# A recurrent cell with a mixture of experts: error rows from transposed predictions, the second hidden state in one operation, history entries and history products moved

## The chip, the cores and the metric

The kernel runs on one core of one Trainium2 chip. The metric is the time on the device, in microseconds (us), of one execution. The core's engines run side by side, each through its own list of instructions, and meet only at semaphores: TensorE (PE, with its weight loads as PEld), VectorE (DVE), ScalarE (ACT), GpSimd (POOL) and SyncE (SP), which here only issues DMA transfers.

## The reference

2048 sequences of 256 steps go through a recurrent cell. A step needs the state, the error and the memory that earlier steps left, so the steps follow one another.

```python
encoded = tanh(xt @ We + st @ Ue + be)                    # 24 values
new_state = tanh(xt @ Wx[c] + st @ Ws[c] + bk[c])         # 8 candidates of 32 values
mem = concatenate([[encoded, err], mem[:, :-1]])          # the 20 last entries of 25 values
a = relu(mem.reshape(b, -1) @ enc_w1 + enc_b1)            # 64
agent_in = relu(a @ enc_w2 + enc_b2)                      # 16
h1, c1 = lstm_cell(agent_in, h1, c1, ...)                 # 16
h2, c2 = lstm_cell(h1, h2, c2, ...)
gate = softmax(h2 @ gate_w + gate_b)                      # 8
theta = clamp01(mean(abs(mem[:, :10, -1])) * 2.5)         # of the 10 last errors
gate = gate * theta + gs * (1 - theta)
st = sum over c of gate[c] * new_state[c]
pred = clamp01(st[:, -1]); err = pred - yt                # pred is the output
```

## The kernel before

The 2048 sequences are two groups of 1024 (8 tiles of 128). An item is one step of one group, so there are 512 items, taken in turn: group 0, group 1, group 0 of the next step, and so on. An item's successor in its own group is two items later. `run_phases` (line 162) writes, for every engine, one phase an item: two phases ahead of the loop, 51 turns of 10 phases (5 steps of both groups, 510 phases), two behind it. A phase of an engine works on three items: `new`, `cur` (the one before) and `old` (two before). The order in which an engine's `phase` function calls its parts is its order of instructions; nothing else sets it.

What one phase of each engine does:

- TensorE (line 447). The memory product (`a_ps`) is the largest part: 12 pairs of `history` matmuls (line 359; a pair is the two column halves of the array, run beside each other) for the older entries, in four steps `kk` of three `PIECES`, spread over two phases so that they lie between parts that wait. `history_waits` (line 352) waits until the entry of the group's last step is in `hist`. Then `state_transpose` (line 289, tiles of 128x128), `encoded_s` (313), `logit_bias` and `gate_logits` (422, 430), `encoder1_now` (371: the newest entry straight from `entry`), `bias_of_cell` (393), `encoder2` (382), `candidates_bias` (324), `cell_gates` of cell 0 (406), `candidates_x` and `candidates_s` (333, 342), `encoded_x`, and `cell_gates` of cell 1, which waits for cell 0's h.
- ScalarE (line 588): all tanh and exponentials, the copy of the transposed state out of PSUM (`state_take`), the relu of the error rows (`at_least_zero`, 520), the fp16 high part of the entry (`entry_high`, 526), copies of h (`next_hidden`, 574).
- VectorE (line 832): cell arithmetic (`cell_terms`, `cell_value`, `new_hidden`), softmax, `mix` and `mix_sum` (the weighted sum over the candidates), `errors` (710), `prediction` (820).
- GpSimd (line 964): `gate_in_sbuf`, two quarters of the mix (`mix_quarter`, 911), kept share of the gate, `new_error`, `keep_prediction`, and `entry_low` (923), the fp16 low part of the entry.
- SyncE (line 240): when both parts of the entry of an item are made (semaphore `q_el`, added to by `entry_low`), four DMAs, one for each quarter q, copy `entry_parts` into `hist` (line 271). Every second phase it also fetches history weights, x and y ahead of need.

An entry's way into `hist` is therefore: `encoded_s` on TensorE, tanh and `entry_high` on ScalarE, `entry_low` on GpSimd, four DMAs, and `history_waits` on TensorE one phase later. The error rows reach `entry` by a unit column in `w_ue`: TensorE multiplies the state into rows 96 to 99, ScalarE takes the relu, VectorE the minimum with 1 and the difference from y.

## Time and profile before

| | us |
|---|---|
| median of 3 runs | 5462.91 |
| lowest, highest | 5460.96, 5463.51 |
| the profiled execution, its own time | 5460.57 |
| its span in the profile | 5458.7 |

| engine | busy us | share of the span |
|---|---|---|
| PE | 5391.8 | 99% |
| PEld | 3426.0 | 63% |
| DVE | 4479.8 | 82% |
| ACT | 3807.2 | 70% |
| POOL | 2421.7 | 44% |

The granted clock of TensorE is at its full level (2.4 GHz) in all 40 slices, and all slices look alike, so one phase out of the middle stands for the others. Matmuls are pipelined: a row of the timeline shows each from its start to the end of its results, so neighbours overlap. The chain of waits shows them end to end, which is what adds up to a phase. PE at 99% means that a matmul is always under way, not that the array is never held up between two forms of work.

### The profile page before, as it was taken

How to read it: one execution, taken by the hardware profiler on the slowest of the kernel's cores; microseconds unless marked ns; L12 is line 12 of the kernel's file. 1: busy time of each engine (PE TensorE's matmuls, PEld its weight loads, DVE VectorE, ACT ScalarE, POOL GpSimd, SP SyncE). 2: the span in 40 equal slices, each digit the busy share in tenths (PEclk: the TensorE clock that was granted, in tenths of full speed). 3: DMA queues.
4: the chain of work that ended last, by engine and by line, in shares of the span. 5: the costliest groups of instructions: out<-in, count | busy, mean ns of one | idle time of the engine just before them, and what ended most of it. 6: DMA issues, size and time to landing. Idle time of an engine off the chain costs nothing.

```text
span 5458.7 us, 188210 instructions
## 1 busy us (share of the span) xinstructions
PE 5391.8 (99%) x67584; PEld 3426.0 (63%) x67584; DVE 4479.8 (82%) x12336; ACT 3807.2 (70%) x9729; POOL 2421.7 (44%) x4613
## 2 busy tenths in 40 slices
PE   8999999999999999999999999999999999999998
PEld 5666666666666666666666666666666666666665
DVE  7888888888888888888888888888888888888887
ACT  5777777777767777777777777777777777777775
POOL 3444444444444444444444444444444444444444
PEclk9999999999999999999999999999999999999999
DMA  2111111111111111111111111111111111111111
GB/s 69 29 29 32 29 32 29 32 29 32 29 32 29 32 29 30 31 29 32 29 32 29 32 29 32 29 32 29 30 31 29 32 29 32 29 32 29 32 29 40
DMA packets 299285, 172.38 MB, mean 32 GB/s; under 512 B 156734, under 2 KB 263882, under 8 KB 298714
## 3 DMA queue, kind: packets, MB, share of 16 engines
q1 hardware_dynamic: 293568, 159.42, 11.2%
q8 instruction: 564, 9.24, 0.7%
q10 hardware_dynamic: 5146, 3.66, 0.2%
q14 instruction: 7, 0.06, 0.0%
HBM read 74.65 MB, written 2.10 MB: 14 GB/s over the span
## 4 chain that ended last, share of the span: by engine, by line
PE 95%; DVE 4%; issue 1%; DMA 0%; POOL 0%; ACT 0%; DVEq 0%; ACTq 0%; POOLq 0%
PE a_ps L366 26%; PE chain L417 17%; PE cand_ps L338 9%; PE a_ps L377 9%; PE cand_ps L347 7%; PE chain L310 5%; PE chain L317 4%; PE chain L403 4%; PE chain L293 4%; PE a_ps L388 3%; PE chain L435 3%; PE cand_ps L330 3%; DVE mixed L799 1%; DVE state L817 1%; DVE added L720 1%
## 5 line engine op out<-in xcount | busy, mean ns | idle before, releaser
L366 PE MATMUL a_ps<-hist,w_hist 125*64 125x512 f16 x12288 | 1896.3, 383 | 24.1 <-DMA w_hist<-enc_table 24.1
L817 DVE TENSOR_REDUCE state<-mixed 128x64 f32<-128x512 f32 x2048 | 1353.4, 682 | 34.2 <-POOL mixed L920 0.8
L920 POOL TENSOR_TENSOR mixed<-cand,gate 128x512 f32<-128x512 f32 x1024 | 1281.1, 1272 | 48.6 <-POOL gate L908 12.5
L554 ACT ACTIVATE cand<-cand_ps 128x512 f32<-128x512 f32 x2048 | 1101.8, 593 | 91.1 <-PE cand_ps L347 90.6
L417 PE MATMUL chain<-cell_in,cell_w 128*64 128x128 f32 x16384 | 1120.7, 278 | 19.8 <-DVE cell_in L735 19.8
L886 POOL TENSOR_TENSOR one_theta<-ones,theta 128x8 f32<-128x8 f32 x512 | 103.4, 202 | 2241.0 <-DVE theta L702 2241.0
L417 PEld LDWEIGHTS chain<-cell_in,cell_w 128*64 128x64 f32 x16384 | 889.2, 136 | 271.5 <-DVE cell_in L735 211.8
L366 PEld LDWEIGHTS a_ps<-hist,w_hist 125*64 125x64 f16 x12288 | 681.4, 109 | 536.2 <-issue 141.7
L561 ACT ACTIVATE gates<-chain 128x384 f32<-128x384 f32 x1024 | 502.0, 490 | 726.3 <-PE chain L417 726.1
L735 DVE SCALAR_TENSOR_TENSOR cell_in<-gates,tanh_c 64x128 f32<-64x128 f32 x2048 | 582.5, 284 | 127.0 <-ACT tanh_c L571 113.4
L720 DVE SCALAR_TENSOR_TENSOR added<-gates 128x256 f32<-128x256 f32 x1024 | 537.1, 524 | 141.2 <-ACT gates L561 141.2
L799 DVE TENSOR_TENSOR mixed<-cand,chain 128x1024 f32<-128x1024 f32 x512 | 615.6, 1202 | 0.0
L338 PE MATMUL cand_ps<-w_x,x_sb 32*128 32x256 f32 x8192 | 587.5, 401 | 0.0
L377 PE MATMUL a_ps<-entry,w_now 100*64 100x256 f32 x4096 | 555.7, 390 | 1.4 <-issue 1.2
L926 POOL TENSOR_TENSOR entry_parts<-entry,entry_parts 128x256 f16<-128x256 f32 x512 | 343.5, 671 | 441.5 <-ACT entry_parts L530 441.5
L347 PE MATMUL cand_ps<-w_s,state_t 32*128 32x256 f32 x8192 | 533.4, 374 | 0.0
L571 ACT ACTIVATE tanh_c<-gates 128x128 f32<-128x128 f32 x1024 | 316.6, 309 | 300.8 <-DVE gates L726 300.8
L347 PEld LDWEIGHTS cand_ps<-w_s,state_t 32*128 32x128 f32 x8192 | 420.1, 185 | 22.4
L338 PEld LDWEIGHTS cand_ps<-w_x,x_sb 32*128 32x128 f32 x8192 | 370.3, 184 | 99.2 <-issue 87.9
L403 PE MATMUL chain<-indicator,cell_bias 128*64 128x512 f16 x2048 | 409.4, 380 | 0.0
L536 ACT ACTIVATE a_sb<-a_ps,columns 128x512 f32<-128x512 f32 x512 | 351.7, 687 | 63.1 <-PE a_ps L377 2.8
L770 DVE TENSOR_REDUCE total<-expd 128x8 f32<-128x64 f32 x512 | 112.6, 220 | 303.7 <-ACT expd L586 303.7
(76 smaller groups left out, 6823.8 us busy)
## 6 DMA issues: line engine op xcount, KB each, us to landing
x_sb<-in_x_l SPq DMA_DIRECT2D x260, 256.0 KB, 2.7
hist<-entry_parts SPq DMA_DIRECT2D x2048, 25.0 KB
w_hist<-enc_table SPq DMA_DIRECT2D x258, 128.0 KB, 2.4
y_rows<-in_y_l SPq DMA_DIRECT2D x260, 8.0 KB
ys<-in_y ACTq DMA_DIRECT2D x1, 2048.0 KB, 16.3
preds_out<-preds SPq DMA_DIRECT2D x1, 2048.0 KB, 7.5
cand<-in_encoder ACTq DMA_DIRECT2D x1, 640.0 KB, 3.8
cell_w<-in_cell ACTq DMA_DIRECT2D x2, 256.0 KB, 4.5
```

The costliest lines, as they stand in the source:

```text
L338: nc.tensor.matmul(cand_ps[q][:, NS * hf:NS * hf + NS], x_sb[rows, x_slot(u), g, P * hf:P * hf + P], w_x[rows, :], start=False, stop=False ...
L347: last = nc.tensor.matmul(cand_ps[q][:, NS * hf:NS * hf + NS], state_t[rows, g, P * hf:P * hf + P], w_s[rows, :], start=False, stop=True, ...
L366: nc.tensor.matmul(a_ps[g][ENC * half:ENC * half + ENC, :], w_hist[0:HROWS, w_slot(u), kk, wp, :], hist[0:HROWS, xp, k, at:at + 512], star ...
L377: last = nc.tensor.matmul(a_ps[g][rows, COLS * p:COLS * p + COLS], w_now[0:ER, p, rows], entry[0:ER, g, :], start=False, stop=True, skip_g ...
L403: nc.tensor.matmul(chain[g][rows, :], cell_bias[:, c, rows], indicator[:, :], start=True, stop=False, skip_group_check=True)
L417: last = nc.tensor.matmul(chain[g][rows, P * r:P * r + P], cell_w[c][:, hf, r, :], cell_in[c][:, g, hf, :], start=False, stop=True, skip_g ...
L554: ins = nc.scalar.activation(cand[:, g, q // 2, :, q % 2, :, :].rearrange("p h s c -> p h (s c)"), cand_ps[q][:, :].rearrange("p (h k) -> ...
L720: V.scalar_tensor_tensor(added[c][:, g, :, :], gates[c][:, g, 1:3, :], 1.0, gates[c][:, g, 3:5, :], ALU.add, ALU.mult).then_inc(q_added[c], 1)
L735: last = V.scalar_tensor_tensor(cell_in[1][rows, g, hf, :], gates[c][rows, g, 0, :], 1.0, tanh_c[c][rows, g, :], ALU.add, ALU.mult)
L799: V.tensor_tensor(mixed[:, 1, :, :, :, :].rearrange("p h l s c -> p (h l) s c"), cand[:, g, 1, :, :, :, :].rearrange("p h l s c -> p (h l) ...
L817: V.tensor_reduce(state[:, g, hf, 2 * pair:2 * pair + 2, :], mixed[:, pair, hf, :, :, :], AX, ALU.add)\
L920: G.tensor_tensor(mixed[:, 0, :, q, :, :], cand[:, g, 0, :, q, :, :], over_s, ALU.mult)\
```

## The change

- The predictions (`pred_now`, 128x8, in a new order of its columns) are transposed by TensorE into 4 rows of `cand_ps[0]` (`prediction_transpose`, two transposes of 128x4). `errors` subtracts y from them directly. `at_least_zero`, `clamped` and the unit column in `w_ue` go. VectorE makes the prediction right behind the last `mix_sum`, and `errors` stands ahead of the second cell's h.
- The second cell's h goes into a tile of its own, `h_second`, in one operation over 128 rows (`second_hidden`) where there were two over 64. The logits take two matmuls of 64 columns where there were four of 32. ScalarE copies h into `cell_in[1]` for the next step (`keep_hidden`, two copies); TensorE's `cell_gates` of cell 1 waits for the copies of the group's last step (`q_hkept`).
- TensorE: two of the three history pairs of `cur` between the transposes and `encoded_s` stand behind it, and the first history pairs of `new` (with `history_waits`) stand behind `bias_of_cell` of cell 0. `candidates_bias` has two history pairs behind it, ahead of cell 0, where there was one.
- GpSimd: `entry_low` is made for `cur` and not for `new`, behind the two `mix_quarter`s, and waits for `q_h[0]` of the same item, which is cell 0's h. `new_error` and `keep_prediction` follow it, then the kept share and the weighting.
- ScalarE: `entry_high` stands behind `encoder1`.
- VectorE: the softmax's total and reciprocal stand at the start of the next phase, so that the loop turns while the exponential is awaited.

```diff
+            def prediction_transpose(item):
+                g, n, u = item
+                pe.wait_ge(q_pred, n)
+                pe.wait_ge(q_cand[0], n)
+                for hf in range(HF):
+                    last = nc.tensor.matmul(cand_ps[0][0:Q, P * hf:P * hf + P],
+                                            pred_now[:, g, Q * hf:Q * hf + Q], ident[:, :], is_transpose=True, start=True, stop=True,
+                                            skip_group_check=True)
+                last.then_inc(q_predps, 1)
...
                     state_transpose(cur, 1)
-                    history(cur, 2, 1, 3)
+                    history(cur, 2, 1, 2)
+                    prediction_transpose(cur)
+                    encoded_s(cur)
+                    history(cur, 2, 2, 3)
                     history(cur, 3, 0, 1)
-                    encoded_s(cur)
-                if new:
-                    history_waits(new, extra)
-                    history(new, 0, 0, 1)
-                if cur:
-                    history(cur, 3, 1, 2)
...
                     bias_of_cell(cur, 0)
                 if new:
-                    history(new, 0, 2, 3)
-                    history(new, 1, 0, 2)
+                    history_waits(new, extra)
+                    history(new, 0)
+                    history(new, 1, 0, 1)
                 if cur:
                     encoder2(cur)
                     candidates_bias(cur)
                 if new:
-                    history(new, 1, 2, 3)
+                    history(new, 1, 1, 3)
...
             def entry_low(item):
                 g, n, u = item
                 pool.wait_ge(q_eh, n)
+                pool.wait_ge(q_h[0], n)
                 G.tensor_tensor(entry_parts[:, g, 1, :], entry[:, g, :], entry_parts[:, g, 0, :],
                                 ALU.subtract).then_inc(q_el, 1)
...
                     mix_quarter(old, 0)
                 if cur:
-                    kept_share(cur)
-                    kept_gate(cur)
+                    entry_low(cur)
                 if old:
                     new_error(old, extra)
                     keep_prediction(old, extra)
-                if new:
-                    entry_low(new)
-                if cur:
+                if cur:
+                    kept_share(cur)
+                    kept_gate(cur)
                     weighted_exponentials(cur)
...
-                V.scalar_tensor_tensor(entry[ZR:ER, g, :], clamped[ZR:ER, g, :], 1.0,
-                                       y_rows[ZR:ER, x_slot(u), g, :], ALU.min, ALU.subtract)\
+                V.tensor_tensor(entry[ZR:ER, g, :], cand_ps[0][0:Q, 0:COLS], y_rows[0:Q, x_slot(u), g, :],
+                                ALU.subtract)\
                     .then_inc(q_err, 1)
...
+            def second_hidden(item):
+                g, n, u = item
+                dve.wait_ge(q_tanhc[1], n)
+                dve.wait_ge(q_out_gate[1], n)
+                V.scalar_tensor_tensor(h_second[:, g, :], gates[1][:, g, 0, :], 1.0, tanh_c[1][:, g, :],
+                                       ALU.add, ALU.mult).then_inc(q_h[1], 1)
...
+            def keep_hidden(item):
+                g, n, u = item
+                act.wait_ge(q_h[1], n)
+                for hf in range(HF):
+                    rows = CELL1_OUT[hf]
+                    last = nc.scalar.activation(cell_in[1][rows, g, hf, :], h_second[rows, g, :], ACT.Copy)
+                last.then_inc(q_hkept, 1)
```

How a phase of TensorE reads in the loop, from the transposes of the state to cell 0, before:

```order
L293 MATMUL chain<-ident,state 128x128 x2
L366 MATMUL a_ps<-hist,w_hist 64x512 x6
L317 MATMUL chain<-state_t,w_ue 64x256
L317 MATMUL chain<-state_t,w_ue 36x256
L366 MATMUL a_ps<-hist,w_hist 64x512 x4
L427 MATMUL chain<-gate_bias,ones 64x64 x2
L366 MATMUL a_ps<-hist,w_hist 64x512 x2
L435 MATMUL chain<-gate_w,cell_in 64x2x16 x4
L366 MATMUL a_ps<-hist,w_hist 64x512 x2
L377 MATMUL a_ps<-entry,w_now 64x256 x4
L403 MATMUL chain<-indicator,cell_bias 64x512 x2
L366 MATMUL a_ps<-hist,w_hist 64x512 x6
```

and in the changed kernel (`L376` is the history matmul, `L305` the new transposes, `L445` the logits):

```order
L293 MATMUL chain<-ident,state 128x128 x2
L376 MATMUL a_ps<-hist,w_hist 64x512 x2
L305 MATMUL cand_ps<-ident,pred_now 4x128 x2
L327 MATMUL chain<-state_t,w_ue 64x256 x2
L376 MATMUL a_ps<-hist,w_hist 64x512 x4
L438 MATMUL chain<-gate_bias,ones 64x64 x2
L376 MATMUL a_ps<-hist,w_hist 64x512 x2
L445 MATMUL chain<-gate_w,h_second 64x64 x2
L376 MATMUL a_ps<-hist,w_hist 64x512 x2
L387 MATMUL a_ps<-entry,w_now 64x256 x4
L413 MATMUL chain<-indicator,cell_bias 64x512 x2
L376 MATMUL a_ps<-hist,w_hist 64x512 x8
```

Three history pairs between the transposes and `encoded_s` became one and the new transposes; the six matmuls behind `cell_bias` became eight, and the first of the eight now carries the wait for the entry in `hist`, which the first of the four behind `w_ue` carried before.

A phase of GpSimd in the loop, with the semaphores that each waits for, before:

```order
L908 TENSOR_TENSOR gate<-fresh,kept 128x64 [waits q_kept,q_fresh]
L913 REGISTER_ALU
L920 TENSOR_TENSOR mixed<-cand,gate 128x2x256 [waits q_sum0_0,q_sum1_0,q_cand1,q_keptfrom]
L920 TENSOR_TENSOR mixed<-cand,gate 128x2x256 [waits q_sum0_0,q_sum1_0,q_cand0,q_keptfrom]
L886 TENSOR_TENSOR one_theta<-ones,theta 128x8 [waits q_theta]
L893 TENSOR_TENSOR kept<-gate,one_theta 128x64 [waits q_keptfrom,q_onetheta]
L947 ISA [waits q_errsum,q_pred]
L947 TENSOR_TENSOR err_ring<-pred_now,ys 128x8
L956 REGISTER_ALU [waits q_pred]
L956 COPY preds<-pred_now 128x8
L926 TENSOR_TENSOR entry_parts<-entry,entry_parts 128x256 [waits q_eh]
L900 TENSOR_TENSOR weighted<-expd,theta 128x64 [waits q_exp]
```

and in the changed kernel:

```order
L920 TENSOR_TENSOR gate<-fresh,kept 128x64 [waits q_kept,q_fresh]
L925 REGISTER_ALU
L932 TENSOR_TENSOR mixed<-cand,gate 128x2x256 [waits q_sum0_0,q_sum1_0,q_cand1,q_keptfrom]
L932 TENSOR_TENSOR mixed<-cand,gate 128x2x256 [waits q_sum0_0,q_sum1_0,q_cand0,q_keptfrom]
L939 TENSOR_TENSOR entry_parts<-entry,entry_parts 128x256 [waits q_h0,q_eh]
L963 ISA [waits q_errsum,q_pred]
L963 TENSOR_TENSOR err_ring<-pred_now,ys 128x8
L972 REGISTER_ALU [waits q_pred]
L972 COPY preds<-pred_now 128x8
L898 TENSOR_TENSOR one_theta<-ones,theta 128x8 [waits q_theta]
L905 TENSOR_TENSOR kept<-gate,one_theta 128x64 [waits q_keptfrom,q_onetheta]
L912 TENSOR_TENSOR weighted<-expd,theta 128x64 [waits q_exp]
```

`entry_low` (the row that writes `entry_parts`) moved from the end of a phase to the middle of the next one, and waits for `q_h0` as well.

## Rows read from the trace of the kernel before

**Rows 1.** The page: the chain that ended last, share of the span by engine.

```profile
PE 95%; DVE 4%; issue 1%; DMA 0%; POOL 0%; ACT 0%; DVEq 0%; ACTq 0%; POOLq 0%
```

**Rows 2.** Chain of waits in a middle phase: start us, us, what.

```profile
2009.59 0.94 PE chain L417 x16
...
2014.44 0.39 PE chain L293 x2
2014.83 0.77 PE a_ps L366 x6
2015.60 0.43 PE chain L317 x4
...
2016.71 0.34 PE chain L435 x8
...
2018.42 0.65 PE a_ps L366 x6
2019.07 0.36 PE a_ps L388 x8
2019.42 0.33 PE cand_ps L330 x4
2019.75 0.34 PE a_ps L366 x2
2020.09 0.94 PE chain L417 x16
```

**Rows 3.** Turns: the longest pieces of the whole chain, once a turn or rarer.

```profile
256.41 1.21 DVE mixed L799
...
889.95 1.21 DVE mixed L799
```

**Rows 4.** Timeline, entry of one item (start us, us, engine line operation [idle before]).

```profile
2006.57 0.42 ACT L530 ACTIVATE entry_parts<-entry 100x256 f16<-100x256 f32 x1
...
2007.06 0.67 POOL L926 TENSOR_TENSOR entry_parts<-entry,entry_parts 128x256 f16<-128x256 f32 x1 [0.83 <-ACT entry_parts L530]
...
2007.88 0.81 SPq L271 DMA_DIRECT2D hist<-entry_parts  x1
```

**Rows 5.** Timeline of SyncE: the fourth DMA of that item's entry.

```profile
2010.72 0.80 SPq L271 DMA_DIRECT2D hist<-entry_parts  x1
```

**Rows 6.** Windows: length, busy of PE, PEld, DVE, ACT, POOL, clock, DMA share, GB/s.

```profile
2012.50:2012.60 0.10, 0.10 (x2) 0.09 (x4) 0.10 (x2) 0.06 (x1) 0.00 (x0) 1.00 0.04 10
2012.60:2012.70 0.10, 0.10 (x4) 0.04 (x2) 0.10 (x1) 0.10 (x1) 0.00 (x0) 1.00 0.00 0
2014.60:2014.70 0.10, 0.10 (x2) 0.04 (x1) 0.00 (x0) 0.10 (x1) 0.00 (x0) 1.00 0.26 49
```

**Rows 7.** Timeline of DVE: cell 0's h of the next item.

```profile
2012.50 0.57 DVE L735 SCALAR_TENSOR_TENSOR cell_in<-gates,tanh_c 64x128 f32<-64x128 f32 x2
```

**Rows 8.** History weights: issue in the timeline, and issue to landing.

```profile
2012.65 0.68 SPq L223 DMA_DIRECT2D w_hist<-enc_table  x1
...
w_hist<-enc_table SPq DMA_DIRECT2D x258, 128.0 KB, 2.4
```

**Rows 9.** Timeline at a turn of the loop: DVE, and the one wait of PE.

```profile
2261.63 0.23 DVE L781 TENSOR_TENSOR fresh<-weighted,recip 128x64 f32<-128x64 f32 x1 [0.40 <-DVE recip L775]
...
2266.16 0.57 DVE L735 SCALAR_TENSOR_TENSOR cell_in<-gates,tanh_c 64x128 f32<-64x128 f32 x2
...
2266.79 1.09 PE L417 MATMUL chain<-cell_in,cell_w 128*64 128x128 f32 x16 [0.39 <-DVE cell_in L735]
```

**Rows 10.** Groups of the page: operations removed or added, and their like.

```profile
L735 DVE SCALAR_TENSOR_TENSOR cell_in<-gates,tanh_c 64x128 f32<-64x128 f32 x2048 | 582.5, 284 | 127.0 <-ACT tanh_c L571 113.4
...
L561 ACT ACTIVATE gates<-chain 128x384 f32<-128x384 f32 x1024 | 502.0, 490 | 726.3 <-PE chain L417 726.1
...
L579 ACT ACTIVATE cell_in<-cell_in 64x128 f32<-64x128 f32 x1024 | 308.3, 301 | 12.7
...
L523 ACT ACTIVATE clamped<-chain 4x256 f32<-4x256 f32 x512 | 192.5, 376 | 83.5 <-PE chain L317 51.2
```

More of the change, by code:

```diff
@@ L432, in gate_logits @@
                 pe.wait_ge(q_h[1], n)
-                for hf in range(HF):
-                    for rows in CELL0_OUT:
-                        last = nc.tensor.matmul(chain[g][rows, 0:TILES * C]
-                                                .rearrange("p (a h k) -> p a h k", a=2, h=HF)[:, :, hf, :],
-                                                cell_in[1][:, g, hf, rows], gate_w[:, hf, :],
-                                                start=False, stop=True, skip_group_check=True)
+                for rows in CELL0_OUT:
+                    last = nc.tensor.matmul(chain[g][rows, 0:TILES * C], h_second[:, g, rows], gate_w[:, :],
+                                            start=False, stop=True, skip_group_check=True)
                 last.then_inc(q_logps, 1)
@@ L518, in encoded @@
                                      bias=be_col[0:ZR, 0:1]).then_inc(q_enc, 1)
-            def at_least_zero(item):
-                g, n, u = item
-                act.wait_ge(q_zps, n)
-                nc.scalar.activation(clamped[ZR:ER, g, :], chain[g][ZR:ER, Z_AT:Z_AT + COLS], ACT.Relu)\
-                    .then_inc(q_rl, 1)
             def entry_high(item):
@@ L599, in phase @@
                 if new:
-                    at_least_zero(new)
                     encoded(new)
-                    entry_high(new)
                 if cur:
@@ L607, in phase @@
                     encoder1(new)
+                    entry_high(new)
+                    agent_input(new, 0)
                 if cur:
+                    keep_hidden(cur)
                     next_hidden(cur, 0)
                 if new:
-                    agent_input(new, 0)
                     cell_tanhs(new, 0)
@@ L852, in phase @@
                     mix_sum(old, 1, 1)
+                    prediction(old)
                 if cur:
@@ L943, in new_error @@
                 step, ring = place(item, extra)
-                pool.wait_ge(q_pred, n)
+                pool.wait_ge(q_pred, n + GROUPS)
                 pool.wait_ge(q_errsum, n)
-                pred = pred_now[:, g, :].rearrange("p (j o) -> p j o", o=1)
-                G.tensor_tensor(err_ring[:, tiles, bass.ds(ring, 1)], pred, ys[:, tiles, bass.ds(step, 1)],
-                                ALU.subtract).then_inc(q_ring, 1)
+                pred = pred_now[:, g, :].rearrange("p (h a l) -> p a h l", h=HF, a=2)
+                G.tensor_tensor(by_quarter(err_ring[:, tiles, bass.ds(ring, 1)]), pred,
+                                by_quarter(ys[:, tiles, bass.ds(step, 1)]), ALU.subtract).then_inc(q_ring, 1)
             def keep_prediction(item, extra):
@@ L953, in keep_prediction @@
                 step, ring = place(item, extra)
-                pool.wait_ge(q_pred, n)
-                pred = pred_now[:, g, :].rearrange("p (j o) -> p j o", o=1)
-                G.tensor_copy(preds[:, tiles, bass.ds(step, 1)], pred).then_inc(q_predout, 1)
+                pool.wait_ge(q_pred, n + GROUPS)
+                pred = pred_now[:, g, :].rearrange("p (h a l) -> p a h l", h=HF, a=2)
+                G.tensor_copy(by_quarter(preds[:, tiles, bass.ds(step, 1)]), pred).then_inc(q_predout, 1)
             def turn_start(turn):
@@ L991, in zeros @@
         return np.zeros(shape, np.float32)
-    out = dict(we=zeros(P, ER), ue=zeros(P, ER), wx=zeros(P, NS), ws=zeros(P, NS), bk=zeros(P, HF, NS),
-               encoder=zeros(P, MEM, ENC), now=zeros(P, 2, P), enc2=zeros(P, 2 * H), gate_w=zeros(P, HF, Q, C),
+    out = dict(we=zeros(P, P), ue=zeros(P, P), wx=zeros(P, NS), ws=zeros(P, NS), bk=zeros(P, HF, NS),
+               encoder=zeros(P, MEM, ENC), now=zeros(P, 2, P), enc2=zeros(P, 2 * H), gate_w=zeros(P, 2, HF, 2, C),
                cell0=zeros(P, HF, 4, HALF), cell1=zeros(P, HF, 4, HALF))
@@ L1005, in weights_laid_out @@
         out["ue"][rows, q:ZR:Q] = of("Ue")
-        out["ue"][S * q + S - 1, ZR + q] = 1.0
         out["wx"][rows] = of("Wx").transpose(1, 2, 0).reshape(D_IN, NS)
```

82 lines of the change are left out of this document (40 added, 42 removed).

## Prediction

> **What bounds the kernel now.** I read first the page's chain that ended last: 95% of it is PE, 4% DVE, nothing is DMA or POOL [rows 1]. TensorE never rests, so its list of work sets the time. Next the turns: the same VectorE piece comes at 256.41 and 889.95, six turns apart [rows 3], so a turn takes 633.54 / 6 = 105.59 us and one of its 10 phases 10.559. The loop's 510 phases make 5385 us of the profiled execution's 5460.57; 75.6 lie around them. Inside a turn, cell 0 begins at 2009.59 and again at 2020.09 [rows 2]: 10.50 a phase, so a turn of the loop adds about 0.59. That is seen in rows 9: at a turn VectorE is held 0.40 ahead of `fresh`, its chain runs late, and cell 1's matmuls wait 0.39 for h. Each step below is priced in us a phase, times 510, against 5460.57 (the median of the runs, 5462.91, is 2.3 above that).
>
> Last I follow what is not on the chain but feeds it: the entry of an item. In the kernel before, `entry_low` runs at 2007.06, as soon as `entry_high` is done (2006.57 + 0.42), and the four DMAs start at 2007.88 [rows 4]. The fourth starts at 2010.72 [rows 5]; the last bytes move in the window that ends at 2012.60, and there are none in the next [rows 6]. TensorE needs them one phase later behind `encoded_s` (L317), at 2015.60 + 0.43 = 2016.03 [rows 2]. So there are over 3 us of slack and no wait is seen. This slack is what the change spends.
>
> **The change, part by part.**
>
> *The entry's way into the history.* `entry_low` now stands behind the mixes of the next phase and waits for cell 0's h of its own item. The item whose entry was made at 2006.6 is the one whose cell 0 starts at 2009.59 and whose h ends at 12.50 + 0.57 = 2013.07 [rows 2, 7]: 3.48 after cell 0's start. In turn, TensorE now waits for the entry behind `bias_of_cell` 0, and only then goes on to cell 0 of the next item. That closes a ring of one phase: cell 0, h, `entry_low`, DMAs, history, `encoder2`, cell 0 of the next item. Its length:
>
> - cell 0's start to its h: 3.48.
> - h to the start of `entry_low`: 0.07, the hop from ScalarE's end 2006.99 to POOL's start 2007.06; then 0.67 for the operation [rows 4].
> - its end 2007.73 to the first DMA's start 2007.88: 0.15 [rows 4].
> - the first DMA's start to the last bytes, 2012.60: 4.72 [rows 4 to 6]. Four issues in a row, 0.95 apart, and 1.88 behind the fourth.
> - last bytes to landing (the semaphore): not shown for this transfer. The bound below is 0. The nearest row is the history weights: issued 2012.65, landing 2.4 later, 2015.05, with their bytes mostly over by 2014.70 [rows 6, 8]: 0.35. I take 0.35, up to 0.6 for the high end.
> - landing to TensorE at pace: where PE did wait, h ended at 2266.73 and the 16 matmuls at 2266.79 + 1.09 = 2267.88, 1.15 in all where an unhindered piece has 0.94 [rows 2, 9]: 0.20, between 0.05 and 0.35.
> - from there to cell 0: four history pairs, 0.65 / 3 each, 0.87; `encoder2` 0.36; `candidates_bias` 0.33; two pairs, 0.34 + 0.22: 2.12 [rows 2].
>
> The sum is 3.48 + 0.07 + 0.67 + 0.15 + 4.72 + 0.35 + 0.20 + 2.12 = **11.76** a phase, between 11.26 and 12.11.
>
> What is queued behind the wait: on TensorE everything, since it goes in order. On POOL `entry_low` holds up `new_error`, `keep_prediction`, the kept share and the weighting; the last of these is wanted only behind the exponential, over 3 us later, so nothing waits for that. `entry_high`, now behind `encoder1`, is done long before h. On SyncE the w, x and y DMAs come behind an item's four and are wanted phases later.
>
> The Trainium skill (DMA: Bandwidth & Descriptors, Anatomy of one DMA) puts a fixed cost of about 2.0 us on a DMA, most of it the receipt of the write. By that the fourth would land at 2012.72, 0.12 behind its bytes instead of my 0.35; the ring would be 11.53 and the total 5956. No row here shows this transfer's landing.
>
> *TensorE's own list.* The transposes of the predictions are new. The state's two transposes take 0.39, and the six history matmuls behind them 0.77 where six take 0.65: 0.51 for a trip into another shape of tiles and back [rows 2]. The new pair streams as many columns in a shape of its own again: +0.50. Low bound: `candidates_bias` with 0.33, and 0.12 too much in the pair behind it (0.34 against 0.22), is 0.45 with 0.22 of streaming; two short transposes instead of that are some 0.35. High bound 0.65. The logits, eight passes in 0.34, become four: -0.15, between -0.10 and -0.20. The turn of the loop is covered by the wait for the exponential: -0.06 a phase. History pairs are 12 as before. So TensorE alone needs 10.50 + 0.50 - 0.15 = **10.85** a phase. That is 0.9 less than the ring, so TensorE waits about 0.9 ahead of the history products of every phase, and these terms all disappear in that wait.
>
> *VectorE.* Second h in one operation: -0.28 (group mean 284, one less) [rows 10]. `errors` from PSUM costs what it did; the prediction moves up. VectorE is not late in the ring: cell 0's arithmetic waits for ScalarE, and the new `errors` waits for the transposes but ends before the logits need h. Worth 0 here.
>
> *ScalarE.* `at_least_zero` goes (-0.38), two copies come (+0.60) [rows 10]. They fit where it waits for cell 0: 726 us of waiting in that one group. If that cover went, +0.2. I take 0.
>
> The total: 5460.57 + 510 x (11.76 - 10.559) = 5460.57 + 612.5 = **6073**. With the ring's ends, 5818 and 6252.
>
> **Rivals.**
>
> *A, the ring is not the bound.* If the entry is in `hist` before TensorE gets there, the period is 10.85 and the time 5460.57 + 510 x (10.85 - 10.559) = 5609; with the transposes' bounds 5533 to 5686. For it: TensorE bounds the kernel today. Against it: the ring would have to be 0.9 shorter, and the part from the first DMA to its last byte alone is 4.72.
>
> *B, faster.* The wait is hidden as in A, and the transposes fall into holes that the list has now: two transposes at 0.10 each without a drain (+0.20), -0.15 of logits, -0.15 where `encoder2` (0.36) now waits for ScalarE and gets one more pair ahead of it: 10.40 a phase, 5379. It decides at a ring under 10.4, that is, if the entry took 1.36 less from h to TensorE than the 6.16 of the sum. Against: the same rows as in A, and each change of shape in rows 2 costs something.
>
> *C, no change.* As B, with a drain on either side of the transposes: 10.5 to 10.6 a phase, 5440 to 5480.
>
> *D, the rule of shapes.* The new transposes write 4 rows and so use a quarter of the array's columns; if such a transpose of fp32 took two passes instead of one, it would cost another 0.2: 11.05 a phase for TensorE, 5711 in case A, nothing under the ring. The Trainium skill (TensorEngine Tiling (Array Packing), Restrictions and Gotchas) says that column tiling excludes the transpose mode for fp32; no row of before has such a transpose.
>
> **How the numbers follow.** The ring: 0.78. A with D: 0.12. B: 0.06. C: 0.04. The forecast is the ring's 6073. For 8 in 10 the ring's upper end can be cut a little and A's middle has to come in: 5600 to 6220 leaves out B, C, half of A and a sliver of the ring, about 0.2. A measurement of this kernel can tell some 0.2% from no change (11 us), so faster 0.06, same 0.04, slower 0.90.
>
> **What would show it.** Right: PE's share falls from 99% to some 92%; PE waits for a DMA into `hist`, or without a named cause, 0.9 a phase at the first history row behind `cell_bias`, in all 510 phases; the chain that ended last goes through SP, DMA, POOL and h of cell 0; `entry_parts` on POOL starts 0.07 behind cell 0's h; a turn takes 117 to 118. Wrong: no wait there and a turn near 108 is A, and then the landing or cell 0's way to h was overestimated. If POOL waits for h but TensorE does not wait, I have taken the wrong phase for the entry. If the wait is there but far from 0.9, the unseen terms (landing, pace) or the transposes are off.

## The result and the profile after

The changed kernel takes 5996.25 us (median of four runs, 5995.74 to 5996.74), the kernel before 5461.93 beside it: a ratio of 1.098, 95% interval 1.096 to 1.099, so slower by 534 us. The profiled execution took 5996.69, its span is 5994.8, the granted clock is 2.4 GHz throughout. The forecast was 6073.

The page of the changed kernel first: its engines, the chain that ended last by engine (answering to [rows 1]), and the groups of the history matmul and of `added`, the first of the operations that VectorE does for each cell. Behind the bar stand busy us and mean ns of one, then the idle time ahead and what ended most of it.

```profile
PE 5500.0 (92%) x66560; PEld 3349.5 (56%) x66560; DVE 4314.5 (72%) x11825; ACT 3887.6 (65%) x10241; POOL 2518.7 (42%) x4613
...
PE 28%; SPq 22%; DMA 19%; DVE 9%; ACT 9%; issue 6%; POOL 6%; POOLq 0%; DVEq 0%; ACTq 0%
...
L376 PE MATMUL a_ps<-hist,w_hist 125*64 125x512 f16 x12288 | 1889.2, 386 | 472.4 <-DMA hist<-entry_parts 448.3
...
L729 DVE SCALAR_TENSOR_TENSOR added<-gates 128x256 f32<-128x256 f32 x1024 | 435.9, 426 | 61.3 <-ACT gates L561 4.0
```

PE has fallen from 99% to 92%, and on the chain from 95% to 28%: it is no longer the bound. In its place stand SyncE's issues and a DMA into `hist`. The table of waits (us in all, times, longest) says how often TensorE waits for it:

```profile
PE a_ps L376 <- DMA hist<-entry_parts: 448.3, 509, 1.0
```

That is in 509 of the loop's 510 phases, 0.88 us each time. The history matmul itself costs what it did, 386 ns (383 in before). One phase of the chain that ended last, which answers to [rows 2]: start us, us, what.

```profile
2000.08 0.30 DVE cell_in L744
...
2000.52 0.68 POOL entry_parts L939
...
2001.30 0.81 SPq L271
...
2004.14 2.17 DMA hist<-entry_parts
...
2006.35 1.05 PE a_ps L376 x8
2007.40 0.36 PE a_ps L398 x8
2007.76 0.33 PE cand_ps L340 x4
2008.08 0.55 PE a_ps L376 x4
2008.63 0.90 PE chain L428 x16
...
2009.56 0.49 ACT gates L561
...
2011.63 0.30 DVE cell_in L744
...
2012.94 0.86 SPq L271
```

This is the ring: h of cell 0 (`cell_in` L744), `entry_low` (L939), three issues 0.95 apart (the first is shown) ahead of the fourth DMA, its landing, the eight history matmuls, `encoder2` (L398), `candidates_bias` (L340), four history matmuls, cell 0 (L428), and its h again at 2011.93. The last row is the next phase's first issue; it is needed further below. Two turn marks of the whole chain, as [rows 3] has them for before, give its mean length:

```profile
702.73 2.20 DMA hist<-entry_parts
...
1864.73 2.20 DMA hist<-entry_parts
```

They stand at the same place of their turns and ten turns apart: 1162.00 / 10 = 116.2 us a turn, 11.62 a phase, where before had 105.59 and 10.559. The loop alone explains it: 510 x (11.62 - 10.559) = 541 us; the difference of the profiled executions is 536.

### The profile page after: what moved, and what is told of

Same layout as the page of the kernel before. It is cut to its first block, busy times and chain, and to the rows that moved or that the text cites. A ratio compares the mean times of both kernels' runs of the same rounds, so it can differ in the third digit from the quotient of the medians.

```text
span 5994.8 us, 187699 instructions
## 1 busy us (share of the span) xinstructions
PE 5500.0 (92%) x66560; PEld 3349.5 (56%) x66560; DVE 4314.5 (72%) x11825; ACT 3887.6 (65%) x10241; POOL 2518.7 (42%) x4613
## 3 DMA queue, kind: packets, MB, share of 16 engines
q1 hardware_dynamic: 293568, 159.45, 10.5%
## 4 chain that ended last, share of the span: by engine, by line
PE 28%; SPq 22%; DMA 19%; DVE 9%; ACT 9%; issue 6%; POOL 6%; POOLq 0%; DVEq 0%; ACTq 0%
SPq L271 22%; DMA hist<-entry_parts 18%; PE a_ps L376 14%; PE chain L428 8%; POOL entry_parts L939 6%; DVE cell_in L744 5%; DVE state L833 4%; ACT gates L561 4%; PE a_ps L398 3%; PE cand_ps L340 3%; ACT cell_in L579 3%; ACT gates L566 2%; DVEq L743 0%; POOLq L938 0%; POOLq L961 0%
## 5 line engine op out<-in xcount | busy, mean ns | idle before, releaser
L376 PE MATMUL a_ps<-hist,w_hist 125*64 125x512 f16 x12288 | 1889.2, 386 | 472.4 <-DMA hist<-entry_parts 448.3
L833 DVE TENSOR_REDUCE state<-mixed 128x64 f32<-128x512 f32 x2048 | 1353.2, 682 | 34.2 <-POOL mixed L932 0.8
L376 PEld LDWEIGHTS a_ps<-hist,w_hist 125*64 125x64 f16 x12288 | 632.1, 109 | 1165.7 <-DMA hist<-entry_parts 695.1
L428 PE MATMUL chain<-cell_in,cell_w 128*64 128x128 f32 x16384 | 1090.1, 274 | 0.5 <-DVE cell_in L744 0.3
L939 POOL TENSOR_TENSOR entry_parts<-entry,entry_parts 128x256 f16<-128x256 f32 x512 | 344.6, 673 | 1715.5 <-DVE cell_in L744 1715.5
L428 PEld LDWEIGHTS chain<-cell_in,cell_w 128*64 128x64 f32 x16384 | 937.5, 136 | 227.0 <-issue 141.0
L760 DVE TENSOR_SCALAR cell_in<-a_ps,columns 64x128 f32<-64x128 f32 x512 | 175.5, 343 | 934.1 <-PE a_ps L398 934.1
L543 ACT ACTIVATE cell_in<-a_ps,columns 64x128 f32<-64x128 f32 x512 | 185.8, 363 | 783.4 <-PE a_ps L398 783.4
L387 PE MATMUL a_ps<-entry,w_now 100*64 100x256 f32 x4096 | 529.1, 378 | 0.0
L729 DVE SCALAR_TENSOR_TENSOR added<-gates 128x256 f32<-128x256 f32 x1024 | 435.9, 426 | 61.3 <-ACT gates L561 4.0
L963 POOL TENSOR_TENSOR err_ring<-pred_now,ys 128x8 f32 x512 | 226.1, 442 | 533.8 <-DVE pred_now L841 533.8
L413 PE MATMUL chain<-indicator,cell_bias 128*64 128x512 f16 x2048 | 396.2, 380 | 0.0
```

Source lines behind the costliest of these rows:

```text
L376: nc.tensor.matmul(a_ps[g][ENC * half:ENC * half + ENC, :], w_hist[0:HROWS, w_slot(u), kk, wp, :], hist[0:HROWS, xp, k, at:at + 512], star ...
L387: last = nc.tensor.matmul(a_ps[g][rows, COLS * p:COLS * p + COLS], w_now[0:ER, p, rows], entry[0:ER, g, :], start=False, stop=True, skip_g ...
L428: last = nc.tensor.matmul(chain[g][rows, P * r:P * r + P], cell_w[c][:, hf, r, :], cell_in[c][:, g, hf, :], start=False, stop=True, skip_g ...
L833: V.tensor_reduce(state[:, g, hf, 2 * pair:2 * pair + 2, :], mixed[:, pair, hf, :, :, :], AX, ALU.add)\
L939: G.tensor_tensor(entry_parts[:, g, 1, :], entry[:, g, :], entry_parts[:, g, 0, :], ALU.subtract).then_inc(q_el, 1)
```

## Experiments

Each ran beside the kernel before on its chip, which took 5459.6 to 5460.0. "The ring theory" below is that of the prediction. Its main rival is that TensorE's own longer list, with the new transposes, costs the time.

**The cause put back in one place.** In the changed kernel the one wait of `entry_low` for h is taken out:

```diff
             def entry_low(item):
                 pool.wait_ge(q_eh, n)
-                pool.wait_ge(q_h[0], n)
```

> The changed kernel, with entry_low on GpSimd no longer waiting for cell 0's h (it still stands behind the two mixes). Ring theory: the period of 11.62 us is the ring h of cell 0, entry_low, four DMAs, history products, cell 0. Without the wait entry_low starts when the mixes end, some 1.8 us behind cell 0's start instead of 3.4, and the entry lands about 0.8 ahead of TensorE. TensorE's own list is left: 11.62 less the 1.00 that the wait costs = 10.62 a phase, 5460 + 510 x (10.62 - 10.56) = 5492, between 5470 and 5560. Rival, the new transposes and the new order of TensorE's list are what costs: the time stays near 5996 and the wait for the DMA shrinks without gain.

Measured: 5576.98, ratio 1.0215 (1.0198 to 1.0232). The ring is gone: 419 us come back, and the chain is TensorE's again. But the time is 85 us over the expectation and outside its range. The page's chain and the group of `added`, then two rows of the timeline and two of the chain of this kernel:

```profile
PE 96%; DVE 2%; issue 1%; ACT 1%; DMA 0%; POOL 0%; DVEq 0%; ACTq 0%; POOLq 0%
...
L729 DVE SCALAR_TENSOR_TENSOR added<-gates 128x256 f32<-128x256 f32 x1024 | 559.9, 547 | 61.3 <-ACT gates L561 3.6
```

```profile
2010.40 0.67 POOL L938 TENSOR_TENSOR entry_parts<-entry,entry_parts 128x256 f16<-128x256 f32 x1
2010.70 0.65 DVE L729 SCALAR_TENSOR_TENSOR added<-gates 128x256 f32<-128x256 f32 x1
```

```profile
2002.09 0.05 issue
2002.14 1.09 PE chain L428 x16
```

Without the wait, `entry_low` runs as soon as the mixes are done, which is beside cell 0's arithmetic on VectorE. There `added` takes 0.65 us; in the changed kernel it takes 0.43. Its h comes 0.22 later, and cell 1's sixteen matmuls, which wait for it, show 1.09 plus 0.05 of issue instead of 0.92. One of the two cells' `added` is hit: (547 - 426) x 2 = 0.24 a phase, 124 us over 512, and e4 below, where nothing runs beside it, is 125.6 faster than this kernel. The number of DMAs isn't the reason: e11 below has four and no wait either, but its `entry_low` runs elsewhere, `added` takes 0.43 and the time is 5453. So the wait for h does something useful in this place: it keeps GpSimd off while VectorE works at the cell. Its price was the ring.

**The ring lengthened by a known piece.** `entry_low`'s operation is made twice, first into a tile that nobody reads:

```diff
+                G.tensor_tensor(spare[:, g, :], entry[:, g, :], entry_parts[:, g, 0, :], ALU.subtract)
                 G.tensor_tensor(entry_parts[:, g, 1, :], entry[:, g, :], entry_parts[:, g, 0, :],
                                 ALU.subtract).then_inc(q_el, 1)
```

> The changed kernel with entry_low's operation made twice in a row, the first time into a spare tile (0.67 us more on GpSimd between h and the first DMA). GpSimd is busy 42% of the span. Ring theory: every phase is longer by this operation, 0.67 to 0.70, so 5996 + 510 x 0.69 = 6348 (6330 to 6360), and TensorE's wait for the DMA grows from 1.0 to 1.7. Rival, TensorE's list bounds: no change, 5996, since GpSimd has room.

Measured: 6318.11 (one execution), 322 us more than the changed kernel, 0.63 a phase. Its chain and its wait:

```profile
2008.88 0.04 POOL spare L940
2008.92 0.59 issue
2009.52 0.68 POOL entry_parts L941
```

```profile
PE a_ps L377 <- DMA hist<-entry_parts: 770.1, 510, 1.6
```

The second operation starts 0.64 behind the first, and TensorE's wait grows from 448.3 to 770.1: by 321.8, the whole difference. So 0.63 more work in the ring costs 0.63 a phase, though GpSimd is busy only 42% of the changed kernel's span. The expectation of 6348 was 30 too high, and its range began 12 above the time, because it took 0.69 for the second operation and not the 0.63 to 0.64 at which two of them follow each other.

**The ring in the kernel before, nothing else.** `entry_low` moved as in the change, with its wait; TensorE's list is that of before:

```diff
                 pool.wait_ge(q_eh, n)
+                pool.wait_ge(q_h[0], n)
...
                     mix_quarter(old, 0)
                 if cur:
+                    entry_low(cur)
                     kept_share(cur)
...
-                if new:
-                    entry_low(new)
```

> The kernel before with one part of the change alone: entry_low for cur behind the mixes, with the wait for cell 0's h. TensorE's list is the old one, with the wait for the entry right behind encoded_s, 4.06 us ahead of cell 0 instead of 2.12. Ring theory: 3.30 (cell 0 to h) + 0.14 + 0.68 + 0.12 + 5.01 (first DMA to landing) + 0.04 + 0.18 (getting to pace) + 4.06 = 13.53 a phase, so 5460 + 510 x (13.53 - 10.56) = 6975, between 6850 and 7050. Rival, the late entry costs what it did in the changed kernel: about 1.0 a phase, 5970. Rival, it costs nothing by itself: 5461.

Measured: 7562.88 (one execution). The direction and the place are as expected, the size is not: a phase takes 14.68 and not 13.53 us. The page's group of history matmuls, then pieces of three phases of the chain, and a window (length, busy of PE, PEld, DVE, ACT, POOL, clock, DMA share, GB/s):

```profile
L366 PE MATMUL a_ps<-hist,w_hist 125*64 125x512 f16 x12288 | 2280.0, 452 | 1563.6 <-DMA hist<-entry_parts 1539.5
```

```profile
2012.24 1.06 PE a_ps L366 x4
...
2019.03 0.97 PE chain L417 x16
...
2033.98 0.96 PE chain L417 x16
...
2043.40 0.62 PE a_ps L366 x4
...
2047.45 0.96 PE chain L417 x16
```

```profile
2013.00:2014.00 1.00, 1.00 (x16) 0.71 (x14) 0.00 (x0) 0.00 (x0) 0.00 (x0) 0.50 0.00 0
```

TensorE waits 3.0 us a phase (1539.5 / 510). Behind the wait before 2012.24 it is granted 1.2 GHz (0.50 in the window): four history matmuls take 1.06. Behind the wait before 2043.40 it is granted 2.4 GHz, and they take 0.62. The mean granted clock is 0.895 over the run; in the changed kernel, with a wait of 0.88, and in e2 with 1.51, it stayed at 0.998 to 0.999. The expected ring of 13.53 had all matmuls at the full level, and where they are, it is what the trace shows: from cell 0 at 2033.98 to cell 0 at 2047.45 there are 13.47, and the six phases of this kind between 2000 and 2240 take 13.33 to 13.50. The phases with slow matmuls take 14.8 to 16.2: 14.95 from 2019.03 to 2033.98, and 16.16 for the one before. So the expectation had the ring's length right and lacked the clock. This also shows what TensorE's reordering in the change is worth: it moves the first use of the entry behind `bias_of_cell`, and so shortens the ring from some 13.5 to 11.6.

**The ring shortened by fewer DMAs, the wait for h kept.** Two DMAs (high part, low part) instead of four (one a quarter); the count that TensorE waits for is halved with them:

```diff
-                for q in range(Q):
-                    sp.dma_start(dst[:, :, bass.ds(at[q], COLS)], entry_parts[q:ER:Q, g, :, :])\
-                        .then_inc(s_hist[g], 16)
+                for a in range(2):
+                    sp.dma_start(dst[:, a, bass.ds(at[0], Q * COLS)].rearrange("r (q b) -> r q b", q=Q),
+                                 entry_parts[0:ER, g, a, :]).then_inc(s_hist[g], 16)
```

> The changed kernel with two DMAs for an entry (high part, low part, each 100 rows of 256) in the place of four (a quarter each, both parts). The wait for h stays. Ring theory: two issues of 0.95 fewer, ring 11.62 - 1.89 = 9.73, below TensorE's list, so the time is the list's, 5492 (5470 to 5560); if the larger transfers take 1 us longer to issue and move, the ring is 10.7 and the time 5540. Rival, the wait for h is harmful in itself (GpSimd's order): the time stays above 5900.

Measured: 5451.40, ratio 0.9984 (0.9975 to 0.9994): 545 us less than the changed kernel, 8 less than before and 41 less than expected, below the range of that expectation. Its chain on the page, then one phase of it:

```profile
PE 99%; DVE 0%; issue 0%; DMA 0%; ACT 0%; POOL 0%; ACTq 0%; POOLq 0%; DVEq 0%
```

```profile
2003.19 0.31 PE cand_ps L305 x2
2003.50 0.58 PE chain L327 x4
...
2004.77 0.12 PE chain L445 x4
...
2005.11 0.86 PE a_ps L387 x8
...
2008.29 0.88 PE chain L428 x16
...
2018.84 0.88 PE chain L428 x16
```

Two issues less, 0.945 each, are 1.89 off the ring's 11.62: 9.73, under TensorE's list, and there is no wait for a DMA left. The list is now seen bare: 2018.84 - 2008.29 = 10.55 a phase, against 10.50 in before [rows 2]. The prediction had 10.85 for it, and the expectation, which took it from the changed kernel's wait, 10.62.

**The ring opened on the other side.** The changed kernel with `entry_high` and `entry_low` where they were, no wait for h, four DMAs:

```diff
                     encoded(new)
+                    entry_high(new)
...
                     encoder1(new)
-                    entry_high(new)
...
                 pool.wait_ge(q_eh, n)
-                pool.wait_ge(q_h[0], n)
...
-                if cur:
-                    entry_low(cur)
                 if old:
                     new_error(old, extra)
                     keep_prediction(old, extra)
+                if new:
+                    entry_low(new)
```

> The changed kernel with the entry's parts where they were before (entry_high ahead of the candidates on ScalarE, entry_low for the new item at the end of GpSimd's phase, no wait for h), four DMAs. Ring theory: no ring through h any more, the entry lands 5 us ahead of TensorE. What is left is TensorE's list as in e4: 5451 (5435 to 5480). Rival, entry_high ahead of the candidates makes the softmax late: 5480 to 5560.

Measured: 5453.44, ratio 0.9988 (0.9979 to 0.9998). That is e4's time from the other side, by leaving out one part of the change and keeping all the rest. The moved entry costs 543 us; everything else in the change together is worth -7. The page's chain doesn't help here: it ends on GpSimd and is 72% issue and 26% POOL. That TensorE's list is the bound is read from its busy share, 99%, and from the absence of any wait for a DMA into `hist`, both as in e4.

**What the rest is made of.** The turn of the loop alone, in the kernel before (`totals` and `reciprocals` at the start of the next phase):

```diff
                 if old:
+                    totals(old)
+                    reciprocals(old)
                     fresh_gate(old)
...
                     below_peak(cur)
-                    totals(cur)
-                    reciprocals(cur)
```

> The kernel before with one part of the change: VectorE makes the softmax's total and reciprocal at the start of the next phase, so that its loop turns while it waits for the exponential. The traces of before show one late phase a turn, 105.59 us a turn against ten phases of 10.50, and TensorE's only wait there. Theory: the 0.59 a turn goes, 51 x 0.59 = 30, time 5430 (5425 to 5440). Rival, the lateness of a turn is on TensorE or another engine too: no change beyond 5 us.

Measured: 5441.91, ratio 0.9968 (0.9955 to 0.998): 17.7 us, 0.35 a turn, where 30 were expected. Of the 0.59 that a turn adds [rows 9], some 0.24 stay: e5's trace still has a late cell 1 once a turn, at 2259.98, with 1.09 for its matmuls as in rows 9.

The second h in one operation alone (`second_hidden`, two logit matmuls of 64 columns, `keep_hidden`), in the kernel before:

```diff
-                for hf in range(HF):
-                    for rows in CELL0_OUT:
-                        last = nc.tensor.matmul(chain[g][rows, 0:TILES * C]
-                                                .rearrange("p (a h k) -> p a h k", a=2, h=HF)[:, :, hf, :],
-                                                cell_in[1][:, g, hf, rows], gate_w[:, hf, :],
+                for rows in CELL0_OUT:
+                    last = nc.tensor.matmul(chain[g][rows, 0:TILES * C], h_second[:, g, rows], gate_w[:, :],
```

> The kernel before with one part of the change: the second cell's h in one operation into a tile of its own, logits in two matmuls of 64 columns, two copies on ScalarE. Theory: TensorE's list loses the difference of the logits' pieces, 0.27 to 0.34 before against 0.12 in the two-DMA variant of the changed kernel, 0.15 to 0.22 a phase; time 5461 - 510 x 0.20 = 5360 (5345 to 5385). Rival, the copies put ScalarE ahead of cell 0's tanh late, or VectorE's chain to h is the true bound: the gain does not come, 5440 to 5470, and cell 1's matmuls wait for h in every phase.

Measured: 5483.58, ratio 1.0044 (1.0029 to 1.0059). A miss of 124 us, on the other side of zero. The turn and this h together, e7:

> Both of these parts on the kernel before, with errors, the history products and the entry as before. Theory: the gains add, 30 + 100: 5330 (5315 to 5355). Rival, they share a cover and do not add: over 5360.

Measured: 5465.43, ratio 1.0011 (1.0001 to 1.002). A miss of 135 us. Pieces of e7's chain, then the wait behind them and three rows of its timeline:

```profile
2009.12 0.12 PE chain L437 x4
...
2009.46 0.05 issue
2009.51 1.08 PE a_ps L379 x8
```

```profile
PEld a_ps L379 <- DVE entry L723: 176.2, 512, 0.7
```

```profile
2008.49 0.38 ACT L523 ACTIVATE clamped<-chain 4x256 f32<-4x256 f32 x1 [0.19 <-PE chain L319]
...
2008.89 0.47 ACT L517 ACTIVATE entry<-chain,columns 96x256 f32<-96x256 f32 x1
2008.90 0.46 DVE L723 SCALAR_TENSOR_TENSOR entry<-clamped,y_rows 4x256 f32<-4x256 f32 x1 [0.27 <-ACT clamped L523]
```

The logits fell from 0.34 to 0.12, by more than the prediction's 0.15. TensorE then comes to `encoder1_now` (L379) earlier, but that needs the entry, whose way through the relu (0.38), the tanh (0.47) and VectorE's difference (0.46) has not become shorter: 0.05 of issue and 1.08 stand where before has 0.92 to 0.98. What is saved ahead is waited for behind.

e8 adds the change's order of the history products to e7, without the new transposes: the first pairs of the next item stand behind `bias_of_cell`. Two pairs are left between the state's transposes and `encoded_s`, where e7 has three and the change one and its new transposes.

> As the last one, and TensorE's history products moved as in the change (first pairs of the new item behind bias_of_cell 0, two ahead of cell 0), two pairs between the transposes and encoded_s. No transposes of predictions, entry_low early as before. Theory: in the two-DMA variant each of the two cell products takes 0.06 less than before (0.88 and 0.92 against 0.94 and 0.98), which I put down to this order: 5330 - 510 x 0.1 = 5280 (5260 to 5330). Against the two-DMA variant (5451) it lacks the transposes, which cost 0.31 and 0.15 in encoded_s: 5451 - 235 = 5216 would be the lower end, if the rest of its list stays. Rival, fewer history products between the transposes and encoded_s lay the copy of the state bare: no gain over the last one or a loss.

Measured: 5533.89, ratio 1.0136 (1.012 to 1.0151), the largest miss: 254 us. The chain goes through ScalarE here, and the table of waits has a second place:

```profile
2011.71 0.60 PE chain L319 x2
...
2012.33 0.38 ACT clamped L519
...
2012.73 0.48 ACT entry L513
```

```profile
PEld chain L319 <- ACT state_t L507: 207.6, 512, 1.7
```

In e7 four history pairs lie between `encoded_s` (L319) and `encoder1_now`, in e8 three. From the end of the one to the start of the other the chain has 1.06 in e7 and 1.04 to 1.07 in e8: the entry's way sets this stretch, so the pair that was taken out of it saves nothing and costs its 0.22 where it now stands. That is the same cause, made larger. The other part is the rival of this expectation: `encoded_s` takes 0.57 to 0.60 where e7 has 0.43, and its weight loads wait 207.6 us for ScalarE's copy of the state, 97.1 in e7. Against both, the two cells' matmuls take 0.88 and 0.93 where e7 has 0.95 and 1.06, which is what the expectation put down to this order. In the changed kernel there are four pairs again. e9 takes the relu away: it is e7 without the relu on ScalarE; VectorE reads the error rows from PSUM, as it does in the change. The error's lower clamp is left out of the computation:

```diff
-                V.scalar_tensor_tensor(entry[ZR:ER, g, :], clamped[ZR:ER, g, :], 1.0,
+                V.scalar_tensor_tensor(entry[ZR:ER, g, :], chain[g][ZR:ER, Z_AT:Z_AT + COLS], 1.0,
                                        y_rows[ZR:ER, x_slot(u), g, :], ALU.min, ALU.subtract)\
...
-                    at_least_zero(new)
```

> The kernel before with the turn and the one-operation h (as e7), and the relu of the error rows on ScalarE left out: VectorE takes the minimum and the difference straight from PSUM. The lower clamp of the error in the memory is missing, so the output is not the reference's; the amount of other work is the same. Theory (the logits' 0.2 was gained and given back because TensorE now arrives at encoder1_now before the entry, whose way is encoded_s, relu 0.38, tanh 0.47): without the relu the entry is ready 0.4 earlier, the piece of encoder1_now goes from 1.08 + 0.05 to 0.86, 0.27 a phase: 5465 - 510 x 0.27 = 5327 (5310 to 5360). Rival, the logits' gain was lost elsewhere (VectorE's chain, the copies on ScalarE): above 5430.

Measured: 5313.55, ratio 0.9732 (0.9716 to 0.9748), inside its range.

```profile
2005.22 0.87 PE a_ps L379 x8
```

With the entry made 0.38 earlier, `encoder1_now` takes 0.87, no issue piece stands ahead of it, and the saving of the logits arrives, 152 us against e7. The transposes of the predictions are what makes the relu needless in the change; they cost 0.46 a phase on TensorE, and the two cells' matmuls, 0.88 and 0.92 in e4 against 0.94 and 1.06 in e9, give 0.20 of it back. That is e4's 138 us above e9, and why e4 and e11 end near zero.

**Two better kernels.** The transposes of the predictions stand directly behind those of the state, ahead of the history pair, in e4 (e10) and in e11 (e12):

```diff
                     state_transpose(cur, 1)
-                    history(cur, 2, 1, 2)
                     prediction_transpose(cur)
+                    history(cur, 2, 1, 2)
                     encoded_s(cur)
```

> The two-DMA variant (e4, 5451) with the transposes of the predictions directly behind those of the state, ahead of the history pair. In e4 the list has two returns from a change of shape there: 0.34 for the history pair (0.22 at pace) behind the state's transposes and 0.58 for encoded_s (0.43) behind the predictions'. Theory: one of the two goes, 0.15 a phase, 5451 - 77 = 5375 (5365 to 5400). Rival, the prediction isn't made yet or the copy of the state is what encoded_s waits for: 5440 to 5460.

Measured: **5405.71**, ratio 0.9901 (0.9885 to 0.9918), 1.0% less than the kernel before; it is 6 us above the expected range.

```profile
2007.17 0.23 PE cand_ps L305 x2
...
2007.73 0.56 PE chain L327 x4
```

The transposes fall from 0.31 to 0.23, `encoded_s` from 0.58 to 0.56, a phase from 10.55 to 10.45: 0.09 instead of the 0.15 that was expected.

> As the last one, with the transposes of the predictions directly behind those of the state. Theory: both gains independent of how the entry goes: 5375 (5360 to 5400), the same as e10. Rival as in e10.

Measured: 5408.37, ratio 0.9906 (0.9889 to 0.9922), 8 us above its range. The order of the transposes is worth the same 45 us with either way of opening the ring, so the two edits don't affect each other.

## Why the prediction was right, and where its terms were off

The forecast was a ring of one phase that ends in a wait of TensorE for the entry in `hist`. The trace shows that wait in 509 of 510 phases, 0.88 us each (0.9 was predicted), PE at 92% (some 92%), and the chain through SP, DMA, POOL and h of cell 0. e2 lengthens the ring and the time follows within 1 us of the added wait; e4 and e11 open it in two different places, and both fall to TensorE's list. So the mechanism is shown, not only read. The forecast was 77 us high; 0.14 a phase of it is the ring (11.76 against 11.62, 71 us). Term by term, from the phase of the chain that is shown above, whose sum is 11.55. The mean of ten turns is 11.62 because every second phase is longer: in the turn behind the shown phase they take 11.56 to 11.58 and 11.61 to 11.72 alternately, and none stands out as the loop's own turn. In the longer ones SyncE has fetched history weights, x and y before; its first issue then starts 0.19 behind `entry_low` and takes 0.86 (2012.94 above) in place of 0.10 and 0.81. The prediction had no term for this, and no run took the fetches out.

| term | predicted | measured |
|---|---|---|
| cell 0's start to its h | 3.48 | 3.30 |
| h to `entry_low` | 0.07 | 0.14 |
| `entry_low`, and to the first DMA | 0.67 + 0.15 | 0.68 + 0.10 |
| first DMA to landing | 4.72 + 0.35 | 5.01 |
| landing to pace | 0.20 | 0.22 |
| pace to cell 0 | 2.12 | 2.10 |

- **Cell 0's start to its h** is the largest error. It was taken from a phase of before in which GpSimd's mix still ran, until 2008.88 + 2.50 = 2011.38, when `added` started:

```profile
2008.88 2.50 POOL L920 TENSOR_TENSOR mixed<-cand,gate 128x512 f32<-128x512 f32 x2
...
2011.11 0.55 DVE L720 SCALAR_TENSOR_TENSOR added<-gates 128x256 f32<-128x256 f32 x1
```

  `added` takes 0.55 there and not the 0.43 that it takes in the changed kernel, where the mix is over (2006.31 + 2.50) before cell 0's `added` starts at 2010.08. That is 0.12, for 0.27 us in which the two ran beside each other. The other 0.05 is the cell's matmuls, 0.93 instead of 0.98 from their start to ScalarE's. The prediction copied a duration without asking what ran beside it; the same effect, larger, made e1 miss.
- **The landing.** It was said to be unseen and put at 0.35. From the fourth issue's start to the landing the chain shows 2.17, where the sum has 1.88 + 0.35 = 2.23. In windows of 0.1 us of this trace the bytes end before 2006.00, and the landing is at 2006.31, so it is some 0.3 behind them. The fixed cost of about 2.0 us for a DMA in the Trainium skill (DMA: Bandwidth & Descriptors, Anatomy of one DMA) is 0.17 short of the row here. That section is about DMAs that GpSimd issues, and these are SyncE's; it puts most of the cost behind the last byte, where here some 0.3 of the 2.17 lie.
- **The hop to GpSimd** is 0.14 where the row of before had 0.07: two waits, 0.02 each, and 0.08 of issue between them, in place of one.
- **TensorE's own list** didn't set the time and was off by more than the ring was: 10.85 predicted, 10.55 measured in e4. The trip for the transposes cost 0.31 + (0.58 - 0.43) = 0.46, near the 0.50. The logits gave 0.34 - 0.12 = 0.22, not 0.15; the sixteen matmuls of cell 0 take 0.88 where [rows 2] has 0.94, those of cell 1 0.92 where the chain of before has 0.96 to 0.99, and `encoder1_now` 0.86 where it has 0.92. So rival A, had it come, would have been e4's 5451 and not 5609, and rival C's 5440 to 5480 was the right place for a kernel without the ring. The chances between the rivals rested on the ring alone, so this error changed nothing in the forecast.
- **Rival D** didn't happen. The two transposes of fp32 that write 4 rows take 0.31, and 0.23 in e10, against 0.37 for the two of 128x128, which stream as many columns. The trace also has one row of TensorE for each (x2), as for those of the state, where an fp32 matmul such as those of `encoded_s` has two (x4). So nothing here looks like two passes. The Trainium skill (TensorEngine Tiling (Array Packing), Restrictions and Gotchas) excludes the transpose mode for fp32 under column tiling; this kernel transposes fp32 into 4 rows of PSUM, and whether the array counts as tiled there, no run shows.
- **The turn.** e5 gives 0.35 a turn and not 0.59. Under the ring it made no difference, as was said.
- **Two ends.** The ring's upper end adds up to 11.76 + 0.25 + 0.15 = 12.16 and not 12.11, and rival C's 10.5 gives 5430 and not 5440. Neither touches the forecast.
- **VectorE and ScalarE** were put at 0. Nothing of them is on the chain outside the stretch from cell 0 to its h, but inside it there is more than the cell: a copy of h on ScalarE (`cell_in` L579, 0.31) and 0.50 of a `mix_sum` on VectorE (`state` L833) stand between the cell's operations. Both are in the 3.30, as their like were in the 3.48.

What stays open: why e10 gained 0.09 and not 0.15 a phase. Its `encoded_s` is still at 0.56, now behind a history pair as in before, so its extra over 0.43 isn't the transposes' shape. The trace points to the expectation's rival, ScalarE's copy of the state:

```profile
2018.08 0.20 PEld L327 LDWEIGHTS chain<-state_t,w_ue 128*64 128x64 f32 x4 [0.21 <-ACT state_t L517]
```

The copy ends at 2017.65 + 0.38 = 2018.03, the first weights load 0.05 behind it, and the first matmul starts together with the load; in before the load is 0.05 behind the copy too, but 0.13 ahead of the matmul. In e4 the load is 0.16 behind the copy, so there something else came last. No run moved the copy to show it. Also open is why e6 is slower than before, not only equal: the relu's way explains that the logits' 0.22 is lost, but cell 1's matmuls also take 1.06 there, some 0.08 more than in before, and no run took that apart. (The turn's gain simply adds: e6 and e7 are 18.2 us apart, e5 gave 17.7.)

## What to carry to other kernels

A producer that is moved later must be followed to its consumer once around the loop: if what it now waits for depends on that consumer, the two make a ring whose length is the period, and every issue in it counts in series however idle its engine is. A gain on the engine that bounds the kernel is only real if what it waits for next arrives as much earlier. And a duration copied from a trace holds for what ran beside it there.

## What was not expected of the hardware

- An operation of VectorE with two SBUF inputs slows down beside one of GpSimd: `added` takes 0.43 alone, 0.55 with 0.27 of overlap, 0.65 with 0.37 (GpSimd's ends are rough in a profile). The Trainium skill (SBUF — State Buffer, SBUF: two separate sides) calls this an exclusive lock for a whole instruction; by that `added` in e1, started at 2010.70 beside an operation that ends at 2011.07, would end at 2011.50, and it ended at 2011.35. Two `tensor_reduce` of `state`, with one input each, take 1.28 in the changed kernel while `entry_low` runs, as in before without it. So VectorE is held, but by less than that rule gives.
- TensorE's granted clock stays at 2.4 GHz through a wait of 0.88 or 1.51 us in each phase. Among e3's waits of 3.0 us it is at 1.2 GHz behind those of 3.04 and 2.96 and at 2.4 GHz behind one of 3.08, so the length of the last wait alone doesn't tell the level. A slow phase costs 1.4 to 2.8 us more than one at the full level.
- A DMA's issue costs SyncE the same for 25 rows of 512 columns (0.945 from one to the next) and for 100 rows of 256 (0.93, at 2012.52 and 2013.45 in e4), so two large ones take half the issue time of four small ones.
